# Relative-position products with 128 stationary columns instead of 84, in the first stage of a hybrid network

## The reference

```python
q, k, v = (qkv[0], qkv[1], qkv[2])
attn = jnp.einsum('bqc,bkc->bqk', q * scale, k)
idx = jnp.arange(WS)[:, None] - jnp.arange(WS)[None, :] + (WS - 1)
Rh = rel_pos_h[idx]
Rw = rel_pos_w[idx]
r_q = q.reshape(-1, WS, WS, hd)
rel_h = jnp.einsum('bhwc,hkc->bhwk', r_q, Rh)
rel_w = jnp.einsum('bhwc,wkc->bhwk', r_q, Rw)
attn = (attn.reshape(-1, WS, WS, WS, WS) + rel_h[:, :, :, :, None] + rel_w[:, :, :, None, :]).reshape(-1, N, N)
```

## Time and profile before

| | us |
|---|---|
| timed runs, median of 3 | 1401.24 (1397.11 to 1401.38) |
| profiled execution, its own time | 1398.71 |
| its span | 1396.9 |
| TensorE matmuls busy | 1077.9 (77%), 7858 instructions |
| TensorE weight loads busy | 821.9 (59%), 7859 instructions |
| VectorE busy | 612.5 (44%) |
| ScalarE busy | 435.3 (31%) |
| GpSimd busy | 303.7 (22%) |
| mean granted TensorE clock | 0.862 |

### The profile page before, as it was taken

One profiled execution on the slowest core, in us unless ns is written; L12 is line 12 of the kernel. 1 busy time (PEld: TensorE's weight loads), 2 busy tenths in 40 slices (PEclk: granted clock), 3 DMA queues, 4 the chain that ended last, 5 costly groups with the idle time before them and its releaser, 6 DMA issues. The chain is left out here.

```text
span 1396.9 us, 22443 instructions
## 1 busy us (share of the span) xinstructions
PE 1077.9 (77%) x7858; PEld 821.9 (59%) x7859; DVE 612.5 (44%) x1443; ACT 435.3 (31%) x878; POOL 303.7 (22%) x497
## 2 busy tenths in 40 slices
PE   6895999969987779989972079997474899752991
PEld 5694888855566568879962036665353455441770
DVE  4743655531145646566555024443354577330112
ACT  3651455533222224433210011110233366410330
POOL 4543201111011110000141700000574212114004
PEclk9956999999999889989975579999677799855996
DMA  7446634100230010000047211111133332142644
GB/s 93 116 115 153 154 70 101 35 2 24 68 77 3 0 45 2 1 2 1 2 133 202 79 40 46 56 47 41 42 86 94 110 98 71 33 98 68 172 139 101
DMA packets 121920, 98.45 MB, mean 70 GB/s; under 512 B 32499, under 2 KB 113453, under 8 KB 121197
## 3 DMA queue, kind: packets, MB, share of 16 engines
q1 hardware_dynamic: 114967, 87.30, 24.6%
q0 software_dynamic: 4608, 9.44, 2.4%
q10 hardware_dynamic: 2261, 0.59, 0.2%
HBM read 69.86 MB, written 35.20 MB: 75 GB/s over the span
## 5 line engine op out<-in xcount | busy, mean ns | idle before, releaser
L991 DVE TENSOR_REDUCE l3a_nmax<-l3a_psS 128x2 f32<-128x512 f32 x96 | 62.8, 686 | 40.2 <-PE l3a_psS L845 40.2
L1347 DVE TENSOR_REDUCE l0a_nmax<-l0a_psS 98x2 f32<-98x392 f32 x96 | 54.2, 567 | 54.4 <-PE l0a_psS L1162 50.4
L947 ACT ACTIVATE l3a_PT<-l3a_psST 128x512 f32<-128x512 f32 x96 | 54.8, 596 | 30.8 <-PE l3a_psST L875 30.4
L2615 PEld LDWEIGHTS l2e_psY<-W2T,l2e_HT 128*128 128x128 f32 x320 | 51.5, 190 | 19.2 <-issue 19.1
L2635 ACT ACTIVATE l2e_H<-l2e_psH 128x512 f32<-128x512 f32 x40 | 21.7, 595 | 131.6 <-PE l2e_psH L2597 131.6
L2615 PE MATMUL l2e_psY<-W2T,l2e_HT 128*128 x320 | 57.3, 332 | 4.0 <-issue 2.3
L1297 ACT ACTIVATE l0a_PT<-l0a_psST 98x392 f32<-98x392 f32 x96 | 47.2, 497 | 42.2 <-PE l0a_psST L1204 41.9
L2583 PE MATMUL l2e_psX<-ident,l2e_X 128*128 128x128 f32 x40 | 8.1, 284 | 59.1 <-DMA l2e_X<-xs 59.1
L194 PE MATMUL l3p_psT<-ident,l3p_xn 128*96 128x128 f32 x32 | 8.0, 425 | 49.4 <-DVE l3p_xn L184 49.4
L2080 PE MATMUL l2i_ps<-l2i_D,l2i_A 96*96 96x96 f32 x512 | 44.5, 248 | 0.0
L2080 PEld LDWEIGHTS l2i_ps<-l2i_D,l2i_A 96*96 96x96 f32 x512 | 44.0, 165 | 0.0
(11 more groups left out here) (528 smaller groups left out, 2951.0 us busy)
## 6 DMA issues: line engine op xcount, KB each, us to landing
l3a_QS<-qd SPq DMA_DIRECT2D x72, 64.0 KB, 2.4
l3a_KS<-kd SPq DMA_DIRECT2D x72, 64.0 KB, 2.4
expert_W<-in_L_ffn_w SPq DMA_DIRECT2D x8, 576.0 KB, 4.1
rd<-l0q_r_p SPq DMA_DIRECT2D x24, 168.0 KB
xs<-const_zeros SPq DMA_DIRECT2D x4, 960.0 KB, 10.3
l2e_X<-xs SPq DMA_DIRECT2D x20, 192.0 KB, 2.5
ys<-l2e_Y SPq DMA_DIRECT2D x20, 192.0 KB, 2.0
l0a_QS<-qd SPq DMA_DIRECT2D x54, 64.0 KB
```

Source lines behind the costliest of these rows:

```text
L947: nc.scalar.activation(PT[n % 3][:, s, :], psST[item % 2][:, :], ACT.Exp).then_inc(exp_done, 1)
L991: nc.vector.tensor_reduce(nmax[k % 2][:, TI * u:TI * (u + 1), s], psS[item % 2][:, :].rearrange("p (t k) -> p t k", t=TI), AX.X, ALU.max, ...
L1347: mx = nc.vector.tensor_reduce(nmax[k % 2][0:WQ, 2 * j:2 * (j + 1), s], psS[item % 2][0:WQ, 0:2 * W0].rearrange("p (t k) -> p t k", t=2), ...
L2615: mm = nc.tensor.matmul(psY[:, t * C:(t + 1) * C], HT[b][t][:, mb, :], W2T[:, bass.ds(e * NM + mb, 1), :].rearrange("p a c -> p (a c)"), s ...
```

## The change

Each product reads 128 stationary columns from the same place: the 84 of its own block and the first 44 of the block that follows in memory. It writes 128 rows of PSUM, of which the evacuations still read 84. To make this possible the blocks lie in one flat tile with 44 further columns behind the last one; GpSimd sets these to zero once, and TensorE waits for that.

```diff
-        Rbd, RHW = st.sb("Rbd", [CH, 2, WS, ROWS]), st.sb("RHW", [ROWS, 2, B * T])
+        blocks, RHW = st.sb("Rbd", [CH, 2 * WS * ROWS + P - ROWS]), st.sb("RHW", [ROWS, 2, B * T])
+        Rbd = blocks[:, 0:2 * WS * ROWS].rearrange("p (a i r) -> p a i r", a=2, r=ROWS)
+        wide = lambda axis, i: blocks[:, (axis * WS + i) * ROWS:(axis * WS + i) * ROWS + P]
...
+            nc.gpsimd.memset(blocks[:, 2 * WS * ROWS:], 0.0).then_inc(rbd_rest, 1)
             fills_done = 0
...
-                            mm = nc.tensor.matmul(ps[bank][0:ROWS, col + k * B * cnt:col + (k + 1) * B * cnt], Rbd[:, axis, i0 + k, :],
+                            mm = nc.tensor.matmul(ps[bank][:, col + k * B * cnt:col + (k + 1) * B * cnt], wide(axis, i0 + k),
                                                   free(src, [2 * T, B // 2], [su, 2], [step, cnt]), start=True, stop=True)
...
             pe.wait_ge(rbd_done, 2)
+            pe.wait_ge(rbd_rest, 1)
             pe.wait_ge(q_free, B)
```

More of the change, by code:

```diff
@@ L451, in opening @@
         rev_mm, rev_done, q_mm, q_free, k_mm, k_free, v_mm, v_free, e_free = st.sems("rev_mm rev_done q_mm q_free k_mm k_free v_mm v_free e_free")
-        kb_step, kf_free, v_init, rbd_done, ones_done, pads_done = st.sems("kb_step kf_free v_init rbd_done ones_done pads_done")
+        kb_step, kf_free, v_init, rbd_done, rbd_rest, ones_done, pads_done = st.sems("kb_step kf_free v_init rbd_done rbd_rest ones_done pads_done")
         ps = [psE, nm.psT[0], nm.psT[1], psQ, psK]
```

## The result

The changed kernel is slower. Six timed runs have a median of 1413.15 us (1410.71 to 1418.72); six of the kernel before, taken with them, have 1399.62 (1396.88 to 1401.38). The ratio is 1.0102, with a 95% interval of 1.0079 to 1.0125, which is 11 to 17.5 us. The profiled execution took 1418.72 us (span 1416.9, clock 0.853): it is the slowest of the six, and its difference from the profile before, 20.0 us, is more than the change costs.

The account below looks back on a forecast made before the run. TensorE alone was taken to bound the four rounds; 128-column loads lengthen them from 37.4 to 49.6 us, so 1398.7 + 12.2 = 1410.9, forecast 1411 us, range 1403 to 1416.

Parts of the forecast that it names:

- TensorE alone limits the rounds, and what they lose stands at the end: Four rounds of relative-position products: TensorE busy without a gap, so a microsecond there is one at the end; tail stays 14.3 us.
- All pairs are held by the load, 111 ns at 2.4 GHz and 214 at 1.2: In the rounds, all 256 load-and-matmul pairs take the time of their 128-column load, whatever moves.
- The low bound of 193 ns: Slow pairs at 1.2 GHz cost 193 ns if load and stream overlapped better; then +7.9 us.
- A load of 128 f32 columns is not a cheaper kind: Weight loads on TensorE: f32 takes 190 ns for 128 columns at 2.4 GHz, 165 for 98; only bf16 is cheaper.
- The clock falls at the same 76.65 us: First round, sixteen-column part: 5.5 us at 2.4 GHz hold 50 pairs, the other 206 run at 1.2 GHz.
- the 49.6 of the sum: All four rounds after the change: 5.5 us fast plus 44.1 us slow, 49.6 us against 37.4.
- The small edits cost 0 to 0.2 us and are hidden: GpSimd's memset 0.10 to 0.21 us, covered by other work; TensorE's added wait 0 to 0.1 us; extra result rows nothing.
- The next stage near 135: First matmul of the stage behind the rounds comes near 135 us, from 122.98 before.
- Rival B: Slow rounds: 128 columns keep the clock up or bring it back; rounds 28.4 us, total 1389.7 us; chance 0.12.
- C: Rival: the 128-column f32 load is cheap after all, 3.7 us less in three rounds, 1395 us; chance 0.02.
- D's whole groups of columns: Rival of no visible change: loads go by whole column groups, so 84 cost as much as 128; 1397 to 1403; chance 0.06.
- The sum of +12.2 us: Whole kernel: the rounds' growth from 37.4 to 49.6 us, added to the profiled 1398.7 us, gives 1410.9.

Follow-up runs that it names:

- e2: Changed kernel, but only the 16-column products take 128 stationary columns, the 112-column ones keep 84; 1407.03 us, ratio 1.0051 to the kernel before.
- e3: Changed kernel, but only the 112-column products take 128 stationary columns, the 16-column ones keep 84; 1403.87 us, ratio 1.0035 to the kernel before.
- e4: Changed kernel, but all products take 96 stationary columns; 1399.39 us, ratio 1.0004 to the kernel before.
- e10: The changed kernel again, unchanged, for a second profile; 1409.99 us, rounds 48.7 us.
- e1: Changed kernel with its flat tile, memset and wait, but products take 84 columns again; 1401.38 us against 1399.16, ratio 1.0013.
- e6: Changed kernel (128 columns) with 16-column products put one by one between the long ones in each round; 1412.06 us, ratio 1.0080 to the kernel before.
- e9: The kernel before again, unchanged, for a second profile; 1396.97 us, rounds 34.2 us.
- e8: Kernel before (84 columns), 16-column products put between long ones, all rounds reading q as axis 0 does (rel_w not the reference's); 1400.04 us, ratio 0.9991.
- e11: Kernel before (84 columns), 16-column products put between long ones, both axis-0 rounds ahead of the axis-1 rounds; 1398.75 us, ratio 0.9995.
- e5: Kernel before (84 columns) with 16-column products put one by one between the long ones in each round; 1401.73 us, ratio 1.0021.

## Why the prediction was right

The forecast was 1411 us, the median is 1413.15. Step by step:

- *TensorE alone limits the rounds, and what they lose stands at the end.* Right. TensorE is busy for all of the rounds, the tail stays at 14.3 us, and the ratio's 14 us (11 to 17.5) agree with the rounds' growth.
- *All pairs are held by the load, 111 ns at 2.4 GHz and 214 at 1.2.* Right: 112 and 213. e2, e3 and e4 show that the price goes by the stationary columns, one by one, and not by the moving ones; that it is the load and not the rows written is the one step left to argument. The low bound of 193 ns, load and stream overlapping better, didn't come.
- *A load of 128 f32 columns is not a cheaper kind.* Right. The mean of its kind elsewhere was 190 ns; here it is 192 at 2.4 GHz and 333 at 1.2.
- *The clock falls at the same 76.65 us.* Nearly: 2.1 us into the short products of 128 columns, 5.2 us after the first product (79.9), and 6.5 after it in e10 (78.3); before it was 5.4. That leaves 49.9 and 48.7 us of rounds for the 49.6 of the sum.
- *The small edits cost 0 to 0.2 us and are hidden.* Right within e1's interval.
- *The next stage near 135.* It was 138.9, since the rounds began 3.4 us later in that profile; their length was right.
- *Rival B, 128 columns keep or bring back the clock.* Refuted: in after, e10, e2, e3 and e6 it never came back in the rounds. So is C, with pairs of 213 ns, and D's whole groups of columns (e4).

The forecast lies 2.2 us below the median. 0.9 of that is its base: it added to the one profiled execution, 1398.71 us, and the median of the kernel before is 1399.62. The sum of +12.2 us is 1.3 (by the medians) to 2.1 (by the ratio) too small, and the term that was off is the one I took as known: the 37.4 us of the rounds before. One profile showed it, and in three of six the third round has a spell at 2.4 GHz, with rounds of 34.2 and 34.8 us (36.4 with the 96 columns of e4). Of before, e9 and e1 the mean is (37.4 + 34.2 + 34.8)/3 = 35.5; of after and e10 it is 49.3. The difference, 13.8, agrees with the 13.5 of the medians and the 14.3 of the ratio. The wide kernels with the old order (after, e10, e2, e3) never had this spell in the rounds; so it seems lost with the width, besides each pair's longer time, though four profiles against three of six don't prove it. For e3, 32 long pairs at 2.4 GHz and 96 at 1.2 cost 32 x 0.016 + 96 x 0.020 = 2.4 us by price, and 4.9 (2.1 to 7.8) were measured; the lost spell fits into the rest, but the interval holds 2.4 as well.

The price of a pair at 2.4 GHz, 96 ns for the long ones, was also taken from an axis-0 round alone; in axis 1 it is 193 at either clock. Rival B's 28.4 us of rounds took 111 ns for these too; no wide round of axis 1 ran at 2.4 GHz long enough to show which holds.

Open stays what brings the clock back in the third round of some executions and not of others: the same kernel shows both (before and e9). And whether a copy of q in the order of axis 1, with quicker splits behind it, would gain: e8's profile keeps 2.9 us of its shorter rounds at the next stage's start, and its runs can't tell them from nothing.

## What to carry to other kernels

Where each f32 weight load serves few moving columns, as here 16 to 112, the pair's price goes by the stationary columns: cut them to what is read, and don't fill the array for its own sake. Read from the trace which of load and stream holds a pair before widening either, at both clock levels. And take the time of a stretch before from more than one profile, since a spell at the other clock moved this one by 3 us of 37. The last runs show the same of a gain: follow it from stage to stage before saying that it was lost, and where.

## What the hardware did that was not expected

- The granted clock fell to 0.50 during the rounds in every profile, in all but e8 and e11 with TensorE busy without a gap, and stayed there through 45 us of unbroken work in the changed kernel (79.9 to 124.6). Within the rounds it returned only with at most 96 columns, in three of six profiles, in the third round, soon after or within long products 187 ns apart.
- f32 matmuls whose 112 moving columns lie 14 floats apart take 193 ns a pair at 2.4 GHz as at 1.2; with neighbouring floats 96 (e5, e8).
- A pair held by its f32 load costs about 1.67 ns a stationary column at 1.2 GHz (84, 96, 128: 139, 160, 213 ns).
- The stage behind the rounds, l0a, took 187.8 to 189.1 us in nine profiles and 191.4 to 191.8 in five, with 84 columns (before and e1) as with 128 (e10 and after). Rounds shortened by 3 to 4 us (e8, e11: 33.5, 33.8) are no more than such a difference, and the runs didn't show them.
